# Routed experts on tiles of tokens sorted by group, with the mixture and the activation moved into the first attention

## What is computed

```python
xn = layernorm(x)
s = L0_attn(xn, ...)          # 16 heads of 16, full softmax, q/k/v/o with LoRA updates
g = silu(L0_ffn(xn, ...))     # routed experts, below
x = x + s * g                 # then layer 1: windowed attention and a gated network

# L0_ffn: 32 experts in 4 groups of 8
scores = sigmoid(x @ gate_w.T);  sb = scores + gate_bias
group_scores = top_k(sb.reshape(T, 4, 8), 2).sum(-1)
gmask = one_hot(top_k(group_scores, 2))         # 2 of 4 groups
topi = top_k(where(gmask, sb, -inf), 8)         # 8 experts out of these 16
cw = scores at topi / their sum * 2.5, else 0
x_lat = x @ fc1_w.T                             # 256 -> 128
h = relu2(x_lat @ w1[e].T) * cw[:, e]           # per expert, 128 -> 128
routed = (sum over e of h @ w2[e].T) @ fc2_w.T
shared = relu2(x @ shared_up_w.T) @ shared_down_w.T
return shared + routed
```

## Time and profile before

| what | us |
|---|---|
| median of 3 runs | 3142.89 (3141.05 to 3150.26) |
| the profiled execution, its own time | 3153.16 |
| its span in the profile | 3151.3 |
| TensorE busy | 3018.0 (96%) |
| VectorE busy | 2118.1 (67%) |
| ScalarE busy | 1862.7 (59%) |
| GpSimdE busy | 1013.5 (32%) |
| first score of the first attention | at 678.85 |

### The profile page before, as it was taken

The page is one execution under the profiler, slowest core; times in us unless marked ns, Lnnn a source line. Parts: engine busy times, 40 slices in busy tenths (PEclk is TensorE's granted clock), DMA queues, the critical chain, the costliest instruction groups (busy, mean ns, idle before and its releaser), DMA issues. The chain is left out here.

```text
span 3151.3 us, 66387 instructions
## 1 busy us (share of the span) xinstructions
PE 3018.0 (96%) x23638; PEld 2264.8 (72%) x23638; DVE 2118.1 (67%) x5888; ACT 1862.7 (59%) x4638; POOL 1013.5 (32%) x1627
## 2 busy tenths in 40 slices
PE   7999999999999999997988999999999999999999
PEld 5888888853444444444877888788887888788887
DVE  5666666678999989984755555655556555565556
ACT  4666666647877777774445555455554555545553
POOL 0000000001100000001016566576655766566653
PEclk9999999988999999998999999999999999999999
DMA  4111111231332232202324434354343543344431
GB/s 150 48 48 48 48 48 41 61 69 31 81 48 55 46 73 35 42 4 89 115 59 111 104 94 99 96 128 103 84 117 87 119 103 93 93 115 110 97 89 44
DMA packets 296483, 246.35 MB, mean 78 GB/s; under 512 B 148956, under 2 KB 231516, under 8 KB 296028
## 3 DMA queue, kind: packets, MB, share of 16 engines
q1 hardware_dynamic: 296156, 242.11, 31.2%
HBM read 100.71 MB, written 44.04 MB: 46 GB/s over the span
## 5 line engine op out<-in xcount | busy, mean ns | idle before, releaser
L1853 ACT ACTIVATE b_pp<-b_pp,b_nm 128x192 f32<-128x192 f32 (+2 forms) x1024 | 472.9, 463 | 452.8 <-DVE b_nm L2020 371.3
L176 DVE TENSOR_REDUCE mx<-ps 128x2 f32<-128x1024 f32 x512 | 622.4, 1224 | 64.4 <-PE ps L167 51.9
L1007 ACT ACTIVATE a_pt<-ps 128x512 f32<-128x512 f32 x1024 | 555.9, 595 | 185.3 <-PE ps L1043 184.3
L1823 POOL TENSOR_SCALAR b_pp<-b_pp,b_rc 128x192 f32<-128x192 f32 x960 | 387.0, 425 | 384.8 <-DVE b_rc L2029 384.8
L2041 DVE COPY b_pt<-ps 128x384 f32<-128x384 f32 (+2 forms) x336 | 181.9, 555 | 317.1 <-PE ps L1942 301.8
L2020 DVE CUSTOM_DVE_ANT_0 b_pp<-ps,b_mk 128x192 f32<-128x192 f32 x960 | 276.3, 353 | 134.9 <-PE ps L1921 134.9
L797 DVE SCALAR_TENSOR_TENSOR f_yac<-ps,f_cw,f_yac 128x128 f32<-128x128 f32 x992 | 277.9, 343 | 125.4 <-PE ps L596 123.0
L596 PEld LDWEIGHTS ps<-w,f_sq 128*128 128x128 f32 x2048 | 265.1, 191 | 26.5 <-issue 6.0
L596 PE MATMUL ps<-w,f_sq 128*128 128x128 f32 x2048 | 270.1, 275 | 0.3
L1976 PE MATMUL ps<-b_wo,b_oT 128*128 128x256 f32 x1024 | 241.6, 380 | 3.7 <-ACT b_vv L1846 3.7
L1056 PE MATMUL ps<-a_pt,a_v 128*32 128x256 f32 x3072 | 242.9, 396 | 0.0
(11 more groups left out here) (282 smaller groups left out, 7335.9 us busy)
## 6 DMA issues: line engine op xcount, KB each, us to landing
b_rt<-b_qf SPq DMA_DIRECT2D x1024, 64.0 KB, 2.0
qk_parts<-f_aa SPq DMA_DIRECT2D x32, 512.0 KB, 2.7
v_rows<-f_va_ SPq DMA_DIRECT2D x16, 512.0 KB, 2.8
rl<-in_W1qT SPq DMA_DIRECT2D x64, 128.0 KB, 2.6
rl<-in_W1kT SPq DMA_DIRECT2D x64, 128.0 KB, 2.6
rl<-in_W1vT SPq DMA_DIRECT2D x32, 256.0 KB, 3.0
b_wo<-in_W1oT SPq DMA_DIRECT2D x16, 512.0 KB, 3.7
b_vs<-b_vv SPq DMA_DIRECT2D x60, 128.0 KB, 2.9
```

The source lines that it names most:

```text
L176: e.tensor_reduce(M["mx"][kh % 3][:, :, jt, h], P.pair(s), AX.X, ALU.max, negate=True).then_inc(P.free_sem(s), 1)
L1007: e.activation(pt[(4 * i + 2 * j + a) % 12][:, :], P.ap((*s, a)), ACT.Exp).then_inc(P.free_sem((*s, a)), 1)
L1823: m = e.tensor_scalar(x, x, r[:, 2 * u + h:2 * u + h + 1], 1.0, ALU.mult, ALU.mult)
L1853: e.activation(x, x, ACT.Exp, bias=nm[n % 4][:, c:c + 1], scale=-1.0, accum_out=sm[n % 4][:, c:c + 1]).then_inc(exp_done, 1)
```

## The change

Tokens are no longer taken chunk by chunk through all experts. The first half now does three things one after the other:

1. Per chunk, everything except the experts. `row` replaces `gate`, `gate_turn`, `latent` and `values`: it computes value, latent and gate columns (416) with the tokens on the partitions. `begin` moves from VectorE to GpSimdE. `sdn` is the shared down product alone; ScalarE copies it to `g`. `rank` counts the tokens of each group so far, with products with a triangular matrix and with ones; GpSimdE splits the weights of a token into those of its two groups. `qk`, `shared` and `sdn` pieces are dealt out behind these steps (`quota`): 7 in each of chunks 1 to 7, 5 in the last routing, 42 behind the places.
2. `places` computes for each token the row in a DRAM table (`slots`) for each of its two groups; each group begins at a multiple of 512. 64 indirect DMAs (`scatter`) on GpSimdE's queue write the rows (128 latents, 8 weights), over zeros that four DMAs wrote at the start.
3. 19 tiles of 512 rows, each with the 8 experts of one group. The group is read from `tile_of` into a register, and 1 MB of weights (w1 and w2 of 8 experts) is loaded per tile, split on ScalarE and GpSimdE (`w_split`). The results go to a DRAM table (`y`).

In the first attention, in slots 8 to 71, each chunk takes eight slots: indirect gathers of both rows of each token on GpSimdE, their sum, transposes, the product with fc2, the sum with the shared part, and x / (1 + exp(-x)) in steps on GpSimdE (bound, + 1, product), ScalarE (exp) and VectorE (reciprocal). `GATE` moves from slot 16 to slot 84. The DMA scratch of GpSimdE is halved (8192). The layout on the host gives w1 and w2 joined per group, and two small tables.

```diff
@@ first_half_plan
+NG = 4
+NT = 19
+NE = E // NG
+RING = 6
...
+        p += [("groups", c - 1)] + quota(1)
+        p += [("row", c, 0), ("chosen", c - 1), ("row", c, 1), ("val", c, 0)] + quota(1)
+        p += [("eight", c - 1), ("row", c, 2), ("val", c, 1)] + quota(1)
+        p += [("weigh", c - 1), ("row", c, 3), ("val", c, 2)] + quota(1)
+        p += [("rank", c - 1), ("val", c, 3)] + quota(3)
...
+    p += quota(1) + [("rank", c)] + quota(1) + [("places",)]
+    p += [("scatter", n) for n in range(32)] + [("w_load", m) for m in range(1)]
+    while behind:
+        p += quota(1)
+    p += [("slots", 0), ("w_split", 0), ("w_load", 1), ("slots", 1), ("lat", 0)]
+    for m in range(NT):
+        p += [("up", m, 0), ("up", m, 1)]
+        for e in range(NE):
+            if m + 1 < NT and e == 1:
+                p.append(("w_split", m + 1))
+            if m + 1 < NT and e == 3:
+                p.append(("lat", m + 1))
+            if e + 2 < NE:
+                p.append(("up", m, e + 2))
...
+            if 0 < m < NT - 1 and e == 5:
+                p.append(("max", m - 1))
...
+            p.append(("down", m, e))
+            if e == NE - 1:
+                p.append(("y_out", m))
+                if m + 2 < NT:
+                    p += [("w_load", m + 2), ("slots", m + 2)]
@@ first_half, sync
+                    w.wait_ge(pool_set, 1)
+                    for i in range(4):
+                        n = NT * GT // 4
+                        e.dma_start(X["slots"][i * n:(i + 1) * n, :].rearrange("(p r) d -> p r d", p=128),
+                                    spread(zero[:, :], 1, n // 128)).then_inc(zero_out, 16)
...
+                elif k == "w_load":
+                    w.wait_ge(pos_ready, 3)
...
+                    if c >= 2:
+                        w.wait_ge(*P.filled(("down", c - 2, NE - 1)))
+                    group = e.value_load(tile_of[0:1, c:c + 1], min_val=0, max_val=NG - 1)
+                    e.dma_start(raw[c % 2][:, :, :].rearrange("p e f -> p (e f)"),
+                                A["w12"][bass.ds(group, 1), :, :].rearrange("a p f -> p (a f)")).then_inc(raw_in[c % 2], 16)
...
+                elif k == "y_out":
+                    w.wait_ge(*P.emptied(("down", c, NE - 1)))
+                    e.dma_start(X["y"][c * GT:(c + 1) * GT, :].rearrange("(i p) d -> p i d", p=128),
+                                y[c % 2]).then_inc(y_out[c % 2], 16)
@@ first_half, pool
+                elif k == "scatter":
+                    w.wait_ge(picked, 2 * NCH)
+                    w.wait_ge(row_act, 4 * NCH)
+                    w.wait_ge(zero_out, 64)
+                    w.wait_ge(pos_ready, 2)
+                    for i in range(2):
+                        e.indirect_dma_start(X["slots"], bass.IndirectOffsetOnAxis(ap=M["pos"][:, i, c:c + 1], axis=0),
+                                             rows[:, c, i, :], None).then_inc(row_out, 16)
@@ first_half, scalar
+                elif k == "w_split":
+                    w.wait_ge(raw_in[c % 2], 16 * (c // 2 + 1))
...
+                    e.activation(w1[0][c % 2], raw[c % 2][:, :, 0:128], ACT.Copy).then_inc(e_high, 1)
@@ first_attention_plan
-GATE = [(s, m, 16 + 20 * m + at) for m in range(2) for s, at in (("load", 0), ("size", 6), ("sum", 8), ("round", 9))]
+GATE = [(s, m, 84 + 20 * m + at) for m in range(2) for s, at in (("load", 0), ("size", 6), ("sum", 8), ("round", 9))]
-    p = [("load_v", 0)]
+    p = [("gather", 0), ("load_v", 0)]
...
+        if 8 <= i < 8 * NCH + 8:
+            x, k = i // 8 - 1, i % 8
+            if k == 0:
+                p.append(("add", x))
+                if x + 1 < NCH:
+                    p.append(("gather", x + 1))
+            elif k == 2:
+                p.append(("tail_turn", x))
+            elif k in (3, 4):
+                p.append(("mix", x, k - 3))
+            elif k == 5:
+                p += [("ex", x, y) for y in range(2)]
+            elif k == 7:
+                p += [("silu", x, y) for y in range(2)]
@@ first_attention, pool
+                    for i in range(4):
+                        for x in range(2):
+                            at = M["pos"][:, x, 4 * n + i:4 * n + i + 1]
+                            e.indirect_dma_start(yk[n % 2][:, x, i, :], None, X["y"],
+                                                 bass.IndirectOffsetOnAxis(ap=at, axis=0)).then_inc(yk_in[n % 2], 16)
@@ first_attention, vector
+                elif k == "mix":
+                    c = s[1]
+                    x = M["g"][:, 4 * c + 2 * n:4 * c + 2 * n + 2, :].rearrange("p i d -> p (i d)")
+                    w.wait_ge(*P.filled(s))
+                    e.tensor_tensor(x, P.ap(s), x, ALU.add).then_inc(P.free_sem(s), 1)
+                elif k == "silu":
+                    w.wait_ge(up_one, 2 * s[1] + n + 1)
+                    e.reciprocal(ex[n], ex[n]).then_inc(inverted, 1)
```

More of the change, by code:

```diff
@@ L235, in first_half_plan @@
-    begin = range(7, E, 2)
-    tail = {1: [("tail_turn",)], 3: [("mix", 0)], 5: [("mix", 1)]}
-    for c in range(NCH):
+    p = [("load", 0), ("weights",), ("load", 1), ("sums", 0), ("begin", 0)]
+    p += [("w_lora", 2, k) for k in range(2)] + [("w_first",), ("turn", 0, 0), ("turn", 0, 1), ("sums", 1), ("begin", 1)]
+    p += [("w_lora", n, k) for n in (0, 1) for k in range(2)]
+    behind = []
+    for c in range(NCH):
+        for j in range(4):
+            behind += [[("qk", c, j), ("qk_rest", c, j)]]
+            if c:
+                behind += [[("sdn", c - 1, j // 2, j % 2)]]
+            behind += [[("shared", c, j)]]
@@ L238, in first_half_plan, with quota @@
+    behind += [[("sdn", NCH - 1, j // 2, j % 2)] for j in range(4)]
+    def quota(n):
+        out = []
+        for s in behind[:n]:
+            out += s
+        del behind[:n]
+        return out
+    for c in range(NCH):
+        if c:
+            p += [("turn", c, 0), ("turn", c, 1)]
         if c + 2 < NCH:
             p.append(("load", c + 2))
[L240 to L267, removed]
+        if c and c + 1 < NCH:
+            p += [("sums", c + 1), ("begin", c + 1)]
@@ L312, in first_half @@
         P = M["banks"].stage()
-        small = n_max = 0
-        in_chunk = sum(s[0] == "max" for s in plan[:plan.index(("down", NCH - 1, E - 1))])
+        n_small = n_b = n_max = 0
+        begun = sum(s[0] == "max" for s in plan)
         for s in plan:
             if s[0] == "max":
-                x = 6 * (n_max % 2) if s[1] >= in_chunk else 0
-                P.take(s, x, x + 1)
-                n_max += 1
-            elif s[0] == "rows":
-                P.take(s, 4)
-            elif s[0] == "mix_up":
-                if s[3] == 0:
-                    P.take(("mix", *s[1:3]), 2 + s[2])
-            elif s[0] in ("tail_turn", "mix") and s[1] == NCH - 1:
-                if s[0] == "tail_turn":
-                    P.take(s, 5)
-            elif s[0] in ("w_lora", "turn", "gate", "gate_turn", "latent", "qk", "values", "shared", "tail_turn", "mix"):
-                P.take(s, small % 3)
-                small += 1
+                P.take(s, 0, 1)
+            elif s[0] in ("w_lora", "turn", "row", "rank"):
+                P.take(s, n_small % 4)
+                n_small += 1
+            elif s[0] == "places":
+                P.take(s, n_small % 4)
+                n_small += 1
+            elif s[0] in ("qk", "shared"):
+                P.take(s, 4 + n_b % 3)
+                n_b += 1
+            elif s[0] == "sdn" and s[3] == 0:
+                P.take(("sdn", *s[1:3]), 7)
+            elif s[0] in ("lat", "rows"):
+                P.take(s, 2)
@@ L903, in first_attention @@
                 last = 0
-            elif s[0] in ("rows", "one", "two", "three") or s[:2] == ("weights", "sum"):
+            elif s[0] in ("rows", "one", "two", "three", "tail_turn", "mix") or s[:2] == ("weights", "sum"):
                 if last is None:
```

651 lines of the change are left out of this document (407 added, 244 removed).

## The result

The changed kernel takes **3278.74 us** (median of 4 runs, 3275.99 to 3285.11) against 3141.97 us (4 runs, 3135.20 to 3150.26) of the kernel before beside it: ratio 1.0437, 95% interval 1.0406 to 1.0467, 137 us more. The forecast was 3197 us, 54 us more, with a range from 3095 to 3285 us. The sign was right and the time lies just inside the range, but the loss is 2.5 times the forecast one, and that the range holds it is luck: its upper part stood there for rivals that did not come. The profiled execution took 3281.19 us (span 3279.4 us).

A forecast was written before the change was run, and what follows sets the result against it. TensorE was taken to set the pace of the first half's experts, with all three engines full in the first attention; -48 + 68 + 34 = +54 us on 3142.89 us gave 3197 us, range 3095 to 3285 us.

The forecast's parts named there:

- start, chunks, last routing: First half before the scatters: start 48 us, chunks 1 to 7 without experts 126 us, last routing and places 12 us.
- 64 scatters: Indirect DMAs from GpSimdE before the tiles: 1.2 us each, 77 us, of which 11 us bare.
- first scatter to first expert product: Before the tiles: scatters 77 us, filling the pipe 9 us, low clock after the pause 5 us.
- tile period: Expert tiles: 18.9 us each, set by late weights and ScalarE's split; 352 us for 19 tiles.
- one reciprocal: First attention, VectorE: 3.4 us for 512 elements, two per chunk; 2.2 us from below, 4.4 us from above.
- first attention, added: Slots 8 to 71, eight chunks: 68 us of added work, mainly VectorE's, plus 34 us of low clock.
- The step that failed: Scatters in the first half: TensorE's 42 pieces, 66 us, run beside them as cover, leaving 11 us bare.
- hidden: First attention, GpSimdE: eight gathers (9.6 us) and seven passes (some 8 us) fit under a chunk's 30 us.
- (d): First attention stays at half clock from slot 15 to 72 (14.6 us per chunk): +83 us, 3280 us; chance 0.10.
- (b): Clock also falls in every expert tile, which then takes 22.2 us: +60 us, 3257 us; chance 0.22.
- (a): Weights in time at ScalarE's split: 14.9 us per tile, 77 us less, 3120 us; chance 0.26.
- (c): GpSimdE's queue: 2.1 us per scatter, +57 us, 3254 us; chance 0.08.

The follow-up runs named there:

- sync_gathers: Changed kernel with the 64 indirect gathers of the first attention replaced by 16 plain DMAs from SyncE's queue, chip A: 3194.5 us.
- paced_gathers: Changed kernel with the same 64 gathers issued one per slot behind a wait, instead of eight in a row, chip A: 3191.9 us.
- no_reciprocal: Changed kernel with the 16 reciprocals of 512 elements replaced by a multiplication by 0: 3117.0 us on chip A, 3232.4 us when run again on B.
- unchanged3: The changed kernel itself run a third time, nothing edited, chip B: 3276.2 us.
- sync_gathers2: Second run, on chip B, of the changed kernel with plain DMAs on SyncE's queue for the gathers: 3241.6 us.
- w1_early: Changed kernel with the w1 half of a tile's weights loaded a tile earlier, chip B: 3233.4 us.
- tanh_w1: Changed kernel with the activation by tanh, without reciprocal or bound, and the early load of w1, chip B: 3183.8 us.

## Why the prediction was right or wrong

| term | forecast | measured |
|---|---|---|
| start, chunks, last routing | 186 | 190.9 |
| 64 scatters | 77 | 83 |
| first scatter to first expert product | 91 | 135; chip A 90 |
| first half, to the first score | 631 | 673.7; chip A 623 |
| tile period | 18.9 | 18.3 |
| one reciprocal | 3.4 | 3.32 |
| first attention, added | 102 | 127; chip A (sync_gathers, paced_gathers) 92 and 89 |
| stages behind it | 0 | 6 |
| in all | +54 | +137 (median) |

**The step that failed** is in the scatters: "Beside them TensorE has 42 pieces, 66 us, as cover." I costed the DMAs on GpSimdE's queue, and their size was right (1.265 us each for 1.2). I took it that engines which share nothing with them in the code go on beside them. In the result, and on three of four chips, they don't: TensorE's products run, but their signals are held back, so ScalarE, VectorE and then TensorE stand for most of the time until the last scatter is issued. In the 96 us from 190 us TensorE ran 128 products, where no_reciprocal on chip A ran 299. The forecast left 11 us of the scatters bare; with 4 of them the stretch takes 67.3 us, so the others add 68 us, and 23 us on chip A. That is 44 us (135 for 91). The same mechanism in the first attention adds 28 us (887.1 in unchanged3 against 858.9 in sync_gathers2, both on chip B), where I had written "hidden" for the gathers because GpSimdE had time. The 83 us that were missing are, by stages, 43 in the first half, 25 in the first attention, 6 behind it, which no term had, and 10 because the terms were read in a profiled execution that was 10 us above the median to which their sum was applied (84 with rounding). The late increments make 44 and 28 us in the first two stages; the other terms there were together 1 and 3 us too high.

**What held, and what was luck.** The tiles wait for their DMAs: ScalarE for the weights ahead of the split (34.5 + 27.7 us of idle time), as forecast, and TensorE for the rows of the slots (41.9 us), which the forecast did not have and which end at nearly the same time. The period is 0.6 us under the forecast; the forecast's own terms add up to 18.5 us and not 18.9. The 90 us on chip A against 91 are two errors that cancel: the scatters took 83 us for 77, what follows them 7 us for 14. Where (d) has 14.6 us per chunk, 16 half slots at 0.89 us more each are 14.2. The granted clock was 0.96 on average from 330 to 620 us, so rival (b) came only in small part: about 24 of these 290 us were at half clock, for instance behind the wait of 2.64 us at 463.60 us (0.56 from 466 to 469 us). The Trainium skill, page "TensorE: Matmul & The Clock Gate", section "HAM oscillation — how this bites in real kernels", describes tiles that each start at half clock behind their DMA; here the clock was at half behind 7 of the 15 waits between 340 and 620 us, and not in each tile. Rival (a), weights in time, was tried by hand in w1_early: 16.0 us per tile, where I had 14.9; TensorE alone was busy for 14.3 of them, where I had 13.7, and the transposes still waited 1.3 us per tile. In the attention, eight slots with a chunk cost on chip A 35.7 us on average over slots 16 to 71 (sync_gathers), 25.0 without reciprocals, 22.9 before: 10.7 us for reciprocals and clock and 2.1 us for the rest, together 12.8, and the forecast had 8.5 + 4.2 = 12.7. (The stage as a whole added less there, 92 us: its first sixteen slots took 50 us in sync_gathers and 63 in the kernel before.) I had split them at 8.2 for the work and 4.2 for the clock; the edit of no_reciprocal brings the clock back to 1.00 together with the 5.8 us of work, so the two are not parted by it. By the repeat count of 8 in the Trainium skill, page "VectorE: DVE Perf Modes", section "Walkthrough: the 8-slice pipeline in each mode", I had estimated 4.3 us for a reciprocal; the trace has 3.32, and it decides.

**The chances.** No case of mine was the one that came: the sum of the forecast plus a mechanism that I had not listed. Rival (d), 3280 us, gives nearly the measured time, and (b) and (c), 3257 and 3254 us, come within 25 us of it, all for other reasons. (b) is refuted above, (c) by a scatter of 1.27 us and not 2.1, and (d) by the granted clock, 0.77 on average from 720 to 1000 us and not half.

**What stays open**: why the increments are held back on B, C and D and were not on A, whether A would stay so at another time, and why only one gets through in 7 to 18 us while the scatters run. How much of the attention's cost is the clock alone was not parted from the reciprocals. The traces show that it happens and when, and not the path.

## What to carry to other kernels

An indirect DMA on GpSimdE is not free for others because its own queue has room: look in the trace whether engines that wait for TensorE start long after the product has ended, and deal such DMAs out with a wait between them instead of issuing them in a row. Where one run's stage doesn't fit another run's of the same code, run an identical kernel on both chips before explaining the difference by an edit. Two operations of 3.3 us side by side on a full engine can cost the clock too; tanh, which needed no other table on ScalarE, took 0.63 us there in place of each.

## What the runs showed of the hardware

- TensorE's semaphore increments come up to 58 us late while GpSimdE issues indirect DMAs one after another, on chips B, C and D, and not in the four runs on A. With 64 plain DMAs from the same queue, on D, none is late.
- A start of VectorE behind ScalarE came at once meanwhile: the copy at 215.12 us ended at 215.81, and VectorE's subtraction began at 215.84.
- An indirect DMA of 128 rows costs GpSimdE 0.95 us and 0.30 us to the next, for rows of 512 or 544 bytes alike; a plain one of 64 KB 0.54 us (4.30 / 8).
- Tanh and exp on ScalarE needed no table load between them: 16 tanh of 512 elements among the exponentials, 0.63 us each (tanh_w1).
- The granted clock fell to half behind 7 of the 15 waits of TensorE at the tiles' transposes between 340 and 620 us, idle times of 1.9 to 4.4 us.
